# Fewer sequencer instructions in VectorE's part of three graph attention layers: row numbers used as loaded, one wait a block, signals on the work itself

## The reference, cut to what matters

```python
# layers 1 and 3 (H = 4); layer 2 is the same with edge weights, H = 8 and no self loops
xh = (h @ W).reshape(n, H, C)
a_src, a_dst = einsum(xh, att_src), einsum(xh, att_dst)
alpha = leaky_relu(a_src[src] + a_dst[dst], 0.2)
alpha = exp(alpha - segment_max(alpha, dst)[dst])
alpha = alpha / segment_sum(alpha, dst)[dst]
out = segment_sum(xh[src] * alpha[:, :, None], dst)
...
x = layernorm(x + layer(x))          # around each of the four layers
```

## Time and profile before

| | |
|---|---|
| median of 3 runs | 5927.08 us (5918.64 to 5931.12) |
| the profiled execution | 5925.47 us, its span 5923.7 us |
| mean granted TensorE clock | 0.749 of full speed |
| busy share: PE, DVE, ACT, POOL | 55%, 55%, 41%, 39% |
| instructions recorded, all engines | 64720 |

### The profile page before, as it was taken

How to read it: one execution, slowest core, us unless ns; L and a number is a source line. 1 busy time by engine, 2 the same in 40 slices (tenths; PEclk the granted TensorE clock), 3 DMA queues, 4 the chain that set the end, 5 groups by cost and what they waited for, 6 DMA issues and landing times. The chain is left out here.

```text
span 5923.7 us, 64720 instructions
## 1 busy us (share of the span) xinstructions
PE 3257.2 (55%) x16208; PEld 1977.8 (33%) x16208; DVE 3247.8 (55%) x10115; ACT 2411.6 (41%) x5229; POOL 2310.7 (39%) x2409
## 2 busy tenths in 40 slices
PE   2887887514555555562255555555523555565563
PEld 1333353303333333341133333333311334333342
DVE  6998953504544545585155555555822455454576
ACT  1766620114434444443244443444433444443453
POOL 3000002173455454415445445444064545545422
PEclk7999998756777777786577777777756777777786
DMA  2111124221122111101111111111021111112110
GB/s 74 59 59 78 59 84 166 85 62 34 46 47 48 44 46 44 45 22 44 38 47 47 45 47 46 46 46 43 4 53 37 46 45 47 46 45 47 46 25 23
DMA packets 127649, 298.66 MB, mean 50 GB/s; under 512 B 45413, under 2 KB 74973, under 8 KB 123713
## 3 DMA queue, kind: packets, MB, share of 16 engines
q0 software_dynamic: 74976, 155.58, 11.4%
q1 hardware_dynamic: 52320, 139.24, 7.1%
HBM read 241.28 MB, written 53.38 MB: 50 GB/s over the span
## 5 line engine op out<-in xcount | busy, mean ns | idle before, releaser
L1399 POOL DMA_INDIRECT work<-table,lane_src x2184 | 2071.5, 948 | 1992.4 <-PE psum L1553 1100.5
L1496 PE MATMUL psum<-work 128*128 128x396 bf16 (+1 forms) x5850 | 1445.0, 395 | 844.1 <-issue 624.5
L1438 ACT ACTIVATE work<-work,middle_node_number 128x384 f16<-128x384 f16 x1587 | 958.1, 604 | 2003.8 <-DMA work<-table,lane_src 711.7
L1714 DVE TENSOR_TENSOR node_sums<-node_sums,psum 128x136 f32 x2418 | 592.6, 294 | 1444.1 <-remote 854.9
L1553 PE MATMUL psum<-work 128*128 128x136 f32 x4836 | 830.6, 337 | 847.6 <-DVE node_sums L1714 659.9
L1496 PEld LDWEIGHTS psum<-work 128*128 128x128 bf16 x5850 | 649.4, 113 | 1475.2 <-issue 997.0
L1553 PEld LDWEIGHTS psum<-work 128*128 128x128 f32 x4836 | 773.3, 239 | 959.1 <-issue 795.3
L1441 ACT ACTIVATE work<-work 128x384 bf16<-128x384 f16 x1587 | 829.4, 523 | 51.8
L715 PE MATMUL psum<-work 128*128 128x448 f16 x2100 | 460.0, 357 | 48.1 <-DVE node_sums L709 44.9
L744 DVE TENSOR_SCALAR work<-work 128x400 f16<-128x400 f16 x1568 | 462.5, 315 | 0.0
L772 PE MATMUL psum<-work 128*128 128x400 f16 x1568 | 340.3, 341 | 112.0 <-DVE work L744 90.2
(11 more groups left out here) (360 smaller groups left out, 2573.5 us busy)
## 6 DMA issues: line engine op xcount, KB each, us to landing
counts<-work SPq DMA_DIRECT2D x14, 2800.0 KB, 8.2
work<-counts SPq DMA_DIRECT2D x14, 2800.0 KB
work<-table,lane_src POOLq DMA_INDIRECT x2184
work<-spread SPq DMA_DIRECT2D x78, 256.0 KB
work<-masks SPq DMA_DIRECT2D x78, 128.0 KB
work<-source_rows SPq DMA_DIRECT2D x39, 192.0 KB
spread<-node_sums SPq DMA_DIRECT2D x4, 896.0 KB
table<-work SPq DMA_DIRECT2D x10, 330.0 KB
```

Of the source, the lines that this page charges most:

```text
L1399: pool.indirect_dma_start(m.ring[:, s % SLOTS, 0:F + H], None, m.d_table[H], bass.IndirectOffsetOnAxis(ap=m.src[:, s:s + 1], axis=0)).then ...
L1438: act.activation(away, rows_of(g, u), ACT.Abs, bias=m.low_tile[:, hi:hi + 1]).then_inc(far_known, 1)
L1496: mm = pe.matmul(aid_banks[:, k, 0:3 * (F + H)], hot_of(g, u)[:, k * P:(k + 1) * P], m.all_thirds[:, :, hi, 0:F + H], start=(hi == 0), sto ...
L1714: dve.tensor_tensor(to, to, sum_slot(s), ALU.add).then_inc(summed, 1)
```

## The change

Nothing that is computed changes, and no engine but DVE gets another instruction. Four edits:

1. In `add_up` the row numbers are loaded into registers of their own for each block (`places_of`) and used as they are, where before each was copied first.
2. From the third block of a group on (`n > 1`) `add_up` waits once, for the products of the whole block, where before it waited at each of three banks. The first block's and the last block's `add_up` of each group keep the waits by bank.
3. Scan instructions that don't depend on each other are no longer chained: each signals the semaphore for which others wait, and DVE itself waits once for all of them (8 scans in `spread`, 2 carried ones; 2·HL scans in `score`, 4 carried ones; HL is 2 for 4 heads and 4 for 8 heads). The numbers that PE and SP wait for grow to match.
4. A signal rides on the instruction whose end it tells of, and the `engine_nop` behind it goes.

```diff
@@ attend @@
+    phase_no = Phase.count
@@ sync, tensor @@
-                    sp.wait_ge(spread_scanned, g)
+                    sp.wait_ge(spread_scanned, 8 * g)
-                pe.wait_ge(spread_scanned, g + 1)
+                pe.wait_ge(spread_scanned, 8 * (g + 1))
-                pe.wait_ge(spread_carried, g + 1)
+                pe.wait_ge(spread_carried, 2 * (g + 1))
-                pe.wait_ge(maxima_scanned, g + 1)
+                pe.wait_ge(maxima_scanned, 2 * HL * (g + 1))
-                pe.wait_ge(maxima_carried, g + 1)
+                pe.wait_ge(maxima_carried, 4 * (g + 1))
@@ spread @@
-                        chain(dve.tensor_tensor_scan(values[half, q, :], mask(g, "keep")[half], data[:, o * 4 + q, :], 0.0, ALU.mult, ALU.add))
-                dve.engine_nop().then_inc(spread_scanned, 1)
+                        dve.tensor_tensor_scan(values[half, q, :], mask(g, "keep")[half], data[:, o * 4 + q, :], 0.0, ALU.mult, ALU.add
+                                               ).then_inc(spread_scanned, 1)
+                dve.wait_ge(spread_scanned, 8 * (g + 1))
@@ score @@
                 for q in range(HL):
-                    chain(dve.tensor_tensor_scan(ahead[:, q, :], mask(g, "reset_ahead"), alpha[:, q, :], NEG, ALU.add, ALU.max))
-                    chain(dve.tensor_tensor_scan(back[:, q, ::-1], mask(g, "reset_back")[:, ::-1], alpha[:, q, ::-1], NEG, ALU.add, ALU.max))
-                dve.engine_nop().then_inc(maxima_scanned, 1)
+                    dve.tensor_tensor_scan(ahead[:, q, :], mask(g, "reset_ahead"), alpha[:, q, :], NEG, ALU.add, ALU.max).then_inc(maxima_scanned, 1)
+                    dve.tensor_tensor_scan(back[:, q, ::-1], mask(g, "reset_back")[:, ::-1], alpha[:, q, ::-1], NEG, ALU.add, ALU.max
+                                           ).then_inc(maxima_scanned, 1)
+                dve.wait_ge(maxima_scanned, 2 * HL * (g + 1))
...
-                chain(dve.tensor_tensor(alpha, alpha, ahead, ALU.subtract))
-                dve.engine_nop().then_inc(exponents, 1)
+                dve.tensor_tensor(alpha, alpha, ahead, ALU.subtract).then_inc(exponents, 1)
+                dve.wait_ge(exponents, g + 1)
@@ add_up @@
-            def add_up(b):
+            def places_of(lo, n):
+                regs = [dve.alloc_register(f"step_j_{phase_no}_{lo}_{n}_{k}") for k in range(n)]
+                dve.load(regs, m.jrow[0:1, lo:lo + n])
+                return [dve.snap(reg, donate=True, min_val=0, max_val=LAST_ROW) for reg in regs]
+
+            def add_up(b, whole):
+                n = len(steps_of(b))
+                places = places_of(b * U, n)
                 for k, s in enumerate(steps_of(b)):
-                    if k % REGS == 0:
-                        n = min(REGS, len(steps_of(b)) - k)
-                        dve.load(m.j_regs[0:n], m.jrow[0:1, s:s + n])
-                    at = dve.snap(m.j_regs[k % REGS], min_val=0, max_val=LAST_ROW)
-                    if k % PER_BANK == 0:
+                    if k == 0 and whole:
+                        dve.wait_ge(product, steps_of(b)[-1] + 1)
+                    elif k % PER_BANK == 0 and not whole:
                         dve.wait_ge(product, bank_end(s))
                     if s >= 2:
                         dve.wait_ge(summed, s - 1)
-                    to = sums[s % 2][:, bass.ds(at, W)]
+                    to = sums[s % 2][:, bass.ds(places[k], W)]
                     dve.tensor_tensor(to, to, sum_slot(s), ALU.add).then_inc(summed, 1)
@@ the loop over groups and blocks @@
-                        add_up(b - 1)
+                        add_up(b - 1, n > 1)
...
-                add_up(blocks[-1])
+                add_up(blocks[-1], False)
```

More of the change, by code:

```diff
@@ L1591, in spread @@
                 for o in range(2):
-                    chain(dve.tensor_tensor_scan(out[:, o, :], m.row_keep[:, g, 0:GROUP], last[:, o, 0:GROUP], 0.0, ALU.mult, ALU.add))
-                dve.engine_nop().then_inc(spread_carried, 1)
+                    dve.tensor_tensor_scan(out[:, o, :], m.row_keep[:, g, 0:GROUP], last[:, o, 0:GROUP], 0.0, ALU.mult, ALU.add
+                                           ).then_inc(spread_carried, 1)
+                dve.wait_ge(spread_carried, 2 * (g + 1))
                 dve.wait_ge(spread_back, g + 1)
@@ L1604, in score @@
                 dve.wait_ge(scores_turned, g + 1)
-                chain(dve.tensor_tensor(alpha, ps_score[:, 0:wide].rearrange("p (q e) -> p q e", e=P), values[:, 0:HL, :], ALU.add))
-                dve.engine_nop().then_inc(scores_taken, 1)
+                dve.tensor_tensor(alpha, ps_score[:, 0:wide].rearrange("p (q e) -> p q e", e=P), values[:, 0:HL, :], ALU.add).then_inc(scores_taken, 1)
+                dve.wait_ge(scores_taken, g + 1)
                 if weighted:
@@ L1631, in score @@
                 for o in range(2):
[L1632 to L1636, removed]
+                    dve.tensor_tensor_scan(outs[AHEAD][0:HL, o, :], m.row_ahead[0:HL, g, 0:GROUP], lasts[AHEAD][0:HL, o, 0:GROUP], NEG,
+                                           ALU.add, ALU.max).then_inc(maxima_carried, 1)
+                    dve.tensor_tensor_scan(outs[BACK][0:HL, o, ::-1], m.row_back[0:HL, g, 1:GROUP + 1][:, ::-1],
+                                           lasts[BACK][0:HL, o, 1:GROUP + 1][:, ::-1], NEG, ALU.add, ALU.max).then_inc(maxima_carried, 1)
+                dve.wait_ge(maxima_carried, 4 * (g + 1))
                 chain(dve.tensor_tensor(ahead, ahead, back, ALU.max))
@@ L1647, in score @@
                 dve.engine_nop().then_inc(maxima_known, 1)
-                chain(dve.tensor_tensor(alpha, alpha, ahead, ALU.subtract))
-                dve.engine_nop().then_inc(exponents, 1)
+                dve.tensor_tensor(alpha, alpha, ahead, ALU.subtract).then_inc(exponents, 1)
+                dve.wait_ge(exponents, g + 1)
                 if self_loops:
                     chain(dve.tensor_tensor(own, own, ahead, ALU.subtract))
-                    chain(dve.tensor_scalar(own, own, 0.0, None, ALU.min))
-                    dve.engine_nop().then_inc(own_known, 1)
+                    dve.tensor_scalar(own, own, 0.0, None, ALU.min).then_inc(own_known, 1)
+                    dve.wait_ge(own_known, g + 1)
                 chain(dve.tensor_copy(m.old_max[g % 2][:, 0:HL], ahead[:, :, P - 1]))
@@ L1656, in score @@
                     dve.wait_ge(drop_known, g)
-                    chain(dve.tensor_scalar(m.ratio[:, 0:H], ps_drop, 0.0, None, ALU.min))
-                    dve.engine_nop().then_inc(drop_clipped, 1)
+                    dve.tensor_scalar(m.ratio[:, 0:H], ps_drop, 0.0, None, ALU.min).then_inc(drop_clipped, 1)
+                    dve.wait_ge(drop_clipped, g)
                 if self_loops:
                     dve.wait_ge(own_done, g + 1)
-                    chain(dve.tensor_tensor(own, own, over(mask(g, "end").unsqueeze(1), full), ALU.mult))
-                    dve.engine_nop().then_inc(own_masked, 1)
+                    dve.tensor_tensor(own, own, over(mask(g, "end").unsqueeze(1), full), ALU.mult).then_inc(own_masked, 1)
+                    dve.wait_ge(own_masked, g + 1)
                 if g:
```

3 lines of the change are left out of this document (1 added, 2 removed).

## The result

The changed kernel takes 5822.5 us (5813.1 to 5832.5, 4 runs), the kernel before 5928.0 beside it: 0.9825 of it, 95% interval 0.9804 to 0.9846. That is 105 us faster. I had forecast 5877 and a range of 5845 to 5912; the sign was right, the gain twice as large.

What follows compares the result with a forecast made beforehand. POOL's gathers pace three stretches of each full group, so DVE savings count only outside them. Terms 14.4 + 6 + 10.8 + 1.5 + 14.8 + 3 = 50 us, from 5925.5; median 1.6 above: 5877, range 5845 to 5912.

Steps and rivals of the forecast that it cites:

- What bounds the kernel: Three stretches of each full group go at POOL's gather pace, about 23.1 us each; DVE has 12 us to spare in each.
- Part 1: Row-number copies removed in add_up: 0.2 us a block, counting once per group, hidden in POOL-paced stretches; 14 x 0.2 us.
- Part 2: One wait a block in add_up: only delays, mostly under cover; -3 us for the ends of layers (bounds -8 to +4).
- Part 3, the sizes: Unchained scans in spread and score overlap: 0.113 us gained per link, 0.79 us for spread's 8 scans.
- Part 3, where it counts: Savings of spread's 8 scans count in 14 of 39 groups, 14.4 us; they vanish in 20 where PE's transpose is late.
- The stalls shrink: POOL's pause shrinks, or fewer instructions make DVE's fetch stalls rarer: 5605, or 5840 with a tenth of the pauses gone; chance 0.07.
- The gain is taken by PE or ACT: In the scoring chain, savings at lines 1522 and 1626 are lost; 24 us remain at most, 5897 to 5912; chance 0.13.
- The waits by bank mattered: Stalls follow DVE's last adds in add_up, so one wait delays three stretches a group: 80 us slower, 6007; chance 0.05.
- Scans don't overlap: Unchained scans in spread and score gain nothing; only signals and 14 x 0.2 remain: 8 us, 5919; chance 0.13.

Runs made afterwards that it cites:

- e15_before: The kernel before, unchanged, run for its profile on the same chip as the copies-only, one-wait-only and changed kernels; 5929.3 us.

## Why the prediction was off, point by point

- **What bounds the kernel**: right. The stretches are 22.98 us where they were 23.08, and follow POOL: with half the gathers they are 12.1.
- **Part 1**: wrong, and the largest miss. The step that failed is "In the POOL-paced stretches this lengthens a stall and gives nothing", so that the copies count "once per group": I had 2.8 us, alone they bring 64. The spacing was off as well. Without the copies eight adds come 0.036 us closer, not 0.2; the 1.81 us of the changed kernel, which I had forecast as 1.7, comes from the one wait. What I left out is that on these stretches an instruction costs others something even when its own engine is idle.
- **Part 2**: right in sign, short in size. It only delays; alone 11 us slower (5 to 16), where I had at most 8. The sum also treats it oddly: the text counts -3 us for the ends of the layers and the sum adds 3. Read as a cost it would make 44.5 us of the 50.5, further from the result.
- **Part 3, the sizes**: right. Eight scans in 2.77 us, a spacing of 0.336 against the forecast 0.34; the four carried scans, 1.26 us to the next instruction before (2145.17 to 2146.43 in its trace), take 0.86 now. The scans overlap. The eight copies that the Trainium skill tells of (VectorE: DVE Perf Modes, "The DRAIN you can't avoid") took the same time with a semaphore behind each as without; for scans the trace disagrees, 3.59 and 2.77 us. The same section of the Trainium skill says that an instruction that isn't held starts earlier. I passed over that sentence; these scans agree with it.
- **Part 3, where it counts**: wrong. I let the gain of `spread`'s scans vanish in the 20 groups where the transpose came late. In the changed kernel 5 are late. I took PE's lateness as fixed in each group; it goes with how many of PE's results have come out by then (11.7 recorded signals a run instead of 9.9). A part of that gain I did overstate: 30.3 us come back in the wait of line 1701 for PE's nine aid matmuls; it is over 2.5 us in 15 groups, where I had thought of five.
- **The rivals**: "The stalls shrink" had the right sign, at 0.07, and the wrong mechanism: there are as many stalls over 5 us as before (97 and 94), of the same total (1248 and 1241 us). Of "The gain is taken by PE or ACT" those 30.3 us at line 1701 are true, at another line than the rival named; the total is larger all the same. "The waits by bank mattered" and "Scans don't overlap" didn't happen. That the gain was twice the forecast came by a way that the sum didn't have; the sign would have been right by the scans alone.
- **The range** ended at 5845, with every link of the scans counted. No term in it stood for PE's signals coming earlier, though I had written that I couldn't say why they were late. That was the place for a wider range.

Shown, for the sessions near 5930: that instructions on DVE's sequencer slow the kernel though they hold no add up; that the copies are a large part of the gain (64 of 113 us in one session); that PE's results come out after POOL's run of gathers. Not shown: that signals on SyncE do the same, since that edit delays loads too; and how an instruction of one engine holds back the results of another. The Trainium skill (NOTIFIC — the notification-queue block, "7.1 Overflow: three behaviours, one of which stalls the engine") says that the block that writes the trace's records always holds its producers back rather than lose one inside. A record for each instruction and each signal could explain why the number of instructions matters, and then part of this gain would belong to the tracing. That the traces of these sessions lack over half of the semaphore updates makes the recording a suspect, and no more. No run here was made without it, so this stays open, as does what makes one session take 4392 us and another 5930.

## What to carry to other kernels

Before you call an instruction free because its engine waits anyway, look whether another engine's results come out late in the same stretch: there 2418 instructions of 13 ns cost some 45 us, though no add came later behind its wait. A wait that is late by a pattern you can't explain belongs into the range, with its whole size, on both sides. And compare within one session: the change was worth 1.8% in some, and without its second part about 0.3% in another. An experiment that adds instructions to an idle engine should move nothing else: the waits that spread SyncE's signals delayed its loads. The fastest version here is the changed kernel with one signal of PE for a bank of products, 0.9774 of before.

## What the runs showed of the hardware

- In the sessions near 5930, while POOL issues indirect gathers (0.95 us each, one per 1.25), PE's results become visible to others one at a time, 9 to 14 recorded signals in 19.8 us, and the rest together from about 2.8 us after the last gather on (1582.86 to 1585.68 in `e15_before`). In two sessions this did not happen with the same program (4392 us).
- In such a stretch more instructions on DVE's sequencer lower that number: 2418 empty ones from 11.7 to 9.9, and the time rises by 0.8%.
- Unchained scans of 0.42 us overlap by 0.08: spacing 0.336.
- The same kernel left 60962 recorded semaphore updates in a session of 4392 us and 27036 in one of 5929, with 62305 instructions in both.
